# A fused layer norm and gated graph convolution on one core: one load moved, three tiles of the normalisation given to other engines, and the first turns of ScalarE and VectorE in another order

## The chip, the core and the metric

The kernel runs on one core of a Trainium2 chip. The engines of that core that compute here are TensorE (PE in the profile), VectorE (DVE), ScalarE (ACT) and GpSimd (POOL); SyncE (SP) issues nearly all transfers between HBM and SBUF. The metric is the time of one execution on the device in microseconds (us), as the median over runs.

## What is computed

x has 128 graphs of 128 nodes with 128 features, adj one 128x128 matrix of integers for each graph. The weights of the loop relation (W, Wg and two biases) are 128x128 and 1x128.

```python
h = jnp.maximum(_layernorm(x, axis=-1), 0.0)
# _direction(x, W, Wg, b, bg, adj, rel_ids):
    h = x @ W.T
    g = h @ Wg.T
    vals = (h[:, :, None, :] + b) * jax.nn.sigmoid(g[:, :, None, :] + bg)
    onehot = (adj[..., None] == rel_ids).astype(h.dtype)
    return jnp.einsum('bnmr,bmrd->bnd', onehot, vals)
out = _direction(node, W_fwd, Wg_fwd, b_fwd, bg_fwd, adj_mat, rels)              # relations 2 to 40
out = out + _direction(node, W_bwd, Wg_bwd, b_bwd, bg_bwd, adj_t, rels)
out = out + _direction(node, W_loop, Wg_loop, b_loop, bg_loop, adj_t, rel1)      # relation 1
x = x + jax.nn.relu(out)
```

adj holds only 0 and 1 in the drawn inputs, so only relation 1 has entries. The kernel computes that relation alone, sums |adj - 0.5| over all entries, and would run a slow path for all relations behind a branch at the end if the sum said that there are other values. That path doesn't run here.

## The kernel before

The 128 graphs are worked in 32 groups of four. A chunk is two groups: x and adj come in 512 KB chunks (eight graphs, 128x1024 elements), the first chunk of x in two halves. SyncE's queue is written out by hand: x's chunks 0 to 3, then adjacency chunk 0, then x's and adjacency's chunks in turn, and later the stores, each behind a wait for `out_ready`.

For each group g the engines do this:

- VectorE, `row_stats(g)`: two bn_stats passes over two graphs each.
- GpSimd, `coefficients(b)`, once for a batch of groups: variance plus epsilon (`var_eps`), the negated mean (`mean_neg`), and 1/sqrt by a power (`rstd`). The batches are groups 0, 1, 2-3, 4-5, then four groups each (6-9, 10-13, ...); a batch's coefficients wait for the statistics of its last group.
- `normalise(g)`: four 128x128 tiles into `xn`, one instruction each. `POOL_SHARES` says how many of them GpSimd does for the first groups (0, 4, 4, 0, 4, 4), from group 6 on `BATCH_SHARES` (3, 4, 3, 3) by the place in the batch; VectorE does the rest. `xn` has four slots, so group g waits for the turn of group g-4.
- TensorE, `turn_rows(g)`: four transposes into PSUM. ScalarE, `relu_turned(g)`: the relu of it rounded to fp32r, `hT_hi`. VectorE, `low_part(g)`: what the rounding left, `hT_lo`.
- ScalarE, `seed(g)`: writes the biases into the PSUM of the products (128x1024). TensorE, `products(g)`: for each graph hi x w_hi, hi x w_lo, and then lo x w_hi, on top of the biases; it gives h and g at once. The first two kinds wait for `hi_ready` and `seeded`, the last for `hT_ready`.
- ScalarE, `sigmoid(g)`: the gate. VectorE, `messages(g)`: the product h times gate, `vals`.
- ScalarE or GpSimd, `edges(g)`: adjacency to float, `mask`. ScalarE does groups 0 to 3 and each fourth one up to 24.
- TensorE, `aggregate(g)`: mask times vals. VectorE, `output(g)`: relu of it plus x, in place in `x_all`; SyncE stores it.
- ScalarE, `watch(c)`: the sum of |adj - 0.5| of one chunk.

Each engine's order is written by hand. TensorE does, in step t, `turn_rows(t + 2)`, `products(t + 1)`, `aggregate(t)`. GpSimd runs ahead by up to four groups. ScalarE and VectorE have a list of first turns by name and then a loop. Ahead of all that stand the setup of the weights (`turn_weights`, `w_gT`, `w_hi`, `split_weights` for `w_lo`), and matmuls on zeros that keep TensorE busy.

Of the kernel before, what the change touches and what calls it, by code (L numbers as in the profile page):

```python
# [18 lines left out]
def build(nc, x, adj, W_fwd, W_bwd, W_loop, Wg_fwd, Wg_bwd, Wg_loop,  # L19
# [14 lines left out]
    BATCHES = [(0, 0), (1, 1), (2, 3), (4, 5)] + [(g, min(g + 3, GROUPS - 1)) for g in range(6, GROUPS, 4)]  # L34
    BATCH = 4 * GROUP

    POOL_SHARES = (0, 4, 4, 0, 4, 4)

    BATCH_SHARES = (3, 4, 3, 3)
    WATCH_LAG = 3  # L40
# [4 lines left out]
    with ctx:  # L45
# [17 lines left out]
        var_eps = sb("var_eps", [128, BATCH_SLOTS, BATCH])  # L63
        rstd = sb("rstd", [128, BATCH_SLOTS, BATCH])
        mean_neg = sb("mean_neg", [128, BATCH_SLOTS, BATCH])
        minus_half = sb("minus_half", [128, BATCH])
        ident = sb("ident", [128, 128])
        ones = sb("ones", [128, 128])
# [41 lines left out]
        var_ready = sem("var_ready")  # L110
        rstd_ready = sem("rstd_ready")
        mean_ready = sem("mean_ready")
        normed_pool = sem("normed_pool")
        normed_dve = sem("normed_dve")
        turned = sem("turned")
# [86 lines left out]
        def live(g):  # L202
            return 0 <= g < GROUPS
# [11 lines left out]
        def pool_groups(g):  # L215

            return sum(pool_share(k) > 0 for k in range(g))

        def dve_groups(g):
            return sum(pool_share(k) < GROUP for k in range(g))  # L220

        def means_before(b):

# [18 lines left out]
        def _(sp):  # L242
# [19 lines left out]
            load_tile(x_all, x, GROUP, GC, CG - GROUP, x_loaded[0])  # L262
            load_x(1)
            load_x(2)
            load_x(3)
            load_adj(0)
            for c in range(4, LOAD_AHEAD):
                load_x(c)
                load_adj(c - 3)
# [47 lines left out]
        def _(pool):  # L317
# [7 lines left out]
            def coefficients(b):  # L325

                first, last = BATCHES[b]
                s, n = b % BATCH_SLOTS, (last - first + 1) * GROUP
                st = stats[:, s, 0:n // 2, :].rearrange("p k (e f) -> p k e f", e=2)
                pool.wait_ge(stats_ready, b + 1)  # L330
                if b >= BATCH_SLOTS:
                    pool.wait_ge(normed_dve, dve_groups(BATCHES[b - BATCH_SLOTS][1] + 1))
                pool.tensor_scalar(var_eps[:, s, 0:n].rearrange("p (k e) -> p k e", e=2), st[:, :, :, 2],
                                   1.0 / D, EPS, ALU.mult, ALU.add).then_inc(var_ready, 1)
                if means_before(b + 1) > means_before(b):
                    pool.tensor_scalar(mean_neg[:, s, 0:n].rearrange("p (k e) -> p k e", e=2), st[:, :, :, 1],
                                       -1.0, 0.0, ALU.mult, ALU.add).then_inc(mean_ready, 1)
                pool.wait_ge(var_ready, b + 1)
                pool.tensor_tensor(rstd[:, s, 0:n], var_eps[:, s, 0:n], minus_half[:, 0:n], ALU.pow  # L339
                                   ).then_inc(rstd_ready, 1)  # L340

            def normalise(g):

# [50 lines left out]
        def _(act):  # L394
# [21 lines left out]
            def seed(g):  # L416

                s = g % 2
                if g >= 2:
# [3 lines left out]
                    bias_all[:, :, :].rearrange("p a d -> p (a d)").unsqueeze(1)  # L423
                    .to_broadcast([128, GROUP, 2 * D]), ACT.Copy).then_inc(seeded, 1)

            def sigmoid(g):
                s = g % 2
                for graphs, more in parts(g):
# [20 lines left out]
            act.wait_ge(w_turned, 1)  # L449
            nc.scalar.activation(w_gT[:, :], bank[6][:, 128:256], ACT.Copy).then_inc(w_gT_ready, 1)  # L450
            nc.scalar.activation(w_hi[:, 0:D], bank[6][:, 0:D], ACT.Copy).then_inc(w_hi_ready, 1)
            act.wait_ge(bits_set, 1)
            act.wait_ge(bias_ready, 1)
            seed(0)
            act.wait_ge(w_turned, 2)
            nc.scalar.activation(w_hi[:, D:2 * D], bank[7][:, 0:D], ACT.Copy).then_inc(w_hi_ready, 1)
            relu_turned(0)
            seed(1)
            sigmoid(0)
            relu_turned(1)  # L460
            edges(0)
            seed(2)
            relu_turned(2)
            sigmoid(1)
            edges(1)
            edges(2)
            act.wait_ge(half_ready, 1)
            for t in range(1, GROUPS - 1):
                if live(t + 2):
                    relu_turned(t + 2)  # L470
                    seed(t + 2)
                sigmoid(t + 1)
                if t >= WATCH_LAG and (t - WATCH_LAG) % CHUNK == 0:
                    watch((t - WATCH_LAG) // CHUNK)
                if live(t + 2) and mask_by_act(t + 2):
                    edges(t + 2)
                if t == GROUPS - 2:
                    watch(CHUNKS - 2)
# [28 lines left out]
        def _(dve):  # L507
# [84 lines left out]

            row_stats(0)
            row_stats(1)
            normalise(0)
            split_weights(0)
            row_stats(2)
            row_stats(3)
            split_weights(1)
            low_part(0)  # L600
            row_stats(4)
            row_stats(5)
            row_stats(6)
            messages(0)
            low_part(1)
            row_stats(7)
            normalise(3)
            low_part(2)
            messages(1)
            row_stats(8)  # L610
            output(0)
            low_part(3)
            row_stats(9)
            row_stats(10)
            for t in range(2, GROUPS + 1):
                if live(t):
                    messages(t)
                output(t - 1)
                if live(t + 3) and pool_share(t + 3) < GROUP:
                    normalise(t + 3)  # L620
                if live(t + 2):
                    low_part(t + 2)
# [89 lines left out]
        def _(pe):  # L712
# [29 lines left out]
            def turn_rows(g):  # L742
                s = g % 2
                if pool_share(g) > 0:
                    pe.wait_ge(normed_pool, pool_groups(g + 1))
                if pool_share(g) < GROUP:
                    pe.wait_ge(normed_dve, dve_groups(g + 1))
                if g >= 2:
                    pe.wait_ge(hT_ready, g - 1)
# [116 lines left out]
```

## Time and profile before

| | |
|---|---|
| three runs, us | 104.58, 104.6, 105.48 (median 104.6) |
| profiled execution, us | 104.03, of it a span of 102.2 from the first to the last instruction |
| TensorE busy | 95.4 us, 93% of the span; its mean granted clock 0.992 |
| VectorE busy | 90.1 us, 88% |
| ScalarE busy | 88.6 us, 87% |
| GpSimd busy | 85.8 us, 84% |
| moved by transfers | 25.45 MB, mean 249 GB/s |

All four engines are busy for most of the span. An instruction's length and the distance to the next one's start differ: on VectorE and ScalarE the next instruction starts 0.08 to 0.1 us before the last one's recorded end where it has nothing to wait for, and TensorE's matmuls overlap by more. So the working reads distances between starts where it can, and lengths only where there is a single instruction.

### The profile page before, as it was taken

The numbers are of one execution on the slowest core, as the hardware profiler recorded it, in microseconds if no ns is written. First come the engines' busy times: TensorE is split into PE (matmuls) and PEld (weight loads), VectorE is DVE, ScalarE is ACT, GpSimd is POOL, SyncE is SP. The second block draws the span as 40 slices with busy tenths as digits, with TensorE's granted clock in tenths as the row PEclk, the third lists the DMA queues.
The fourth block names the chain that finished last, engine by engine and source line by source line (L and its number), as shares of the span: only waits on it lengthen the run. The fifth ranks groups of instructions, "written<-read, shape, count | busy, mean of one in ns | idle before, by whom it ended". The sixth has DMA issues, their size and how long they took to land.

```text
span 102.2 us, 2493 instructions
## 1 busy us (share of the span) xinstructions
PE 95.4 (93%) x802; PEld 91.3 (89%) x802; DVE 90.1 (88%) x196; ACT 88.6 (87%) x144; POOL 85.8 (84%) x162
## 2 busy tenths in 40 slices
PE   5986899998999999999999999999999999999960
PEld 2655789797999999999999999999999999999950
DVE  2289989999999999999999999999999788777761
ACT  5075498899799998999899989998999989898990
POOL 2188999999999999999999999999999999991000
PEclk9999999999999999999999999999999999999996
DMA  1899999999999999999999999999945150606345
GB/s 50 242 319 292 290 290 290 291 293 294 293 312 298 328 328 331 311 329 322 333 282 317 271 324 316 327 292 313 345 134 157 58 151 28 184 6 205 103 140 168
DMA packets 50288, 25.45 MB, mean 249 GB/s; under 512 B 866, under 2 KB 50276, under 8 KB 50276
## 3 DMA queue, kind: packets, MB, share of 16 engines
q1 hardware_dynamic: 50000, 25.17, 88.5%
q10 hardware_dynamic: 276, 0.13, 0.4%
q8 instruction: 6, 0.10, 0.4%
q14 instruction: 6, 0.05, 0.1%
HBM read 16.91 MB, written 8.39 MB: 247 GB/s over the span
## 4 chain that ended last, share of the span: by engine, by line
PE 71%; POOL 4%; ACT 3%; issue 1%; DVE 0%; POOLq 0%
PE psum L786 23%; PE psum L764 12%; PE psum L769 12%; PE psum L765 12%; PE psum L751 11%; POOL rstd L339 3%; ACT junk L442 2%; POOL xn L352 1%; ACT gate L436 0%; PE psum L811 0%; DVE dist_sum L628 0%; DVE flag L630 0%; POOLq L362 0%
## 5 line engine op out<-in xcount | busy, mean ns | idle before, releaser
L352 POOL TENSOR_SCALAR xn<-x_all,mean_neg,rstd 128x128 f32<-128x128 f32 x101 | 44.7, 454 | 0.7 <-POOL rstd L339 0.4
L764 PE MATMUL psum<-w_hi,hT_hi 128*128 128x256 f32 x128 | 33.8, 299 | 1.3 <-DVE w_lo L589 0.9
L786 PE MATMUL psum<-vals,mask 128*128 128x128 f32 x256 | 33.6, 275 | 0.1
L421 ACT ACTIVATE psum<-bias_all 128x1024 f32<-128x1024 f32 x32 | 33.1, 1035 | 0.3 <-DVE vals L557 0.3
L786 PEld LDWEIGHTS psum<-vals,mask 128*128 128x128 f32 x256 | 31.0, 191 | 0.2 <-issue 0.2
L765 PE MATMUL psum<-w_lo,hT_hi 128*128 128x256 f32 x128 | 31.0, 277 | 0.0
L524 DVE BATCH_NORM_STATS2 stats<-x_all 128x6 f32<-128x256 f32 x64 | 23.9, 418 | 3.2 <-DMA x_all<-in_x 3.0
L764 PEld LDWEIGHTS psum<-w_hi,hT_hi 128*128 128x128 f32 x128 | 24.1, 188 | 2.0 <-DVE w_lo L589 1.1
L557 DVE TENSOR_TENSOR vals<-psum,gate 128x512 f32<-128x512 f32 (+1 forms) x33 | 21.9, 663 | 3.9 <-ACT gate L436 3.3
L339 POOL TENSOR_TENSOR rstd<-var_eps,minus_half 128x16 f32<-128x16 f32 (+2 forms) x11 | 24.5, 2225 | 0.1
L765 PEld LDWEIGHTS psum<-w_lo,hT_hi 128*128 128x128 f32 x128 | 24.2, 189 | 0.0
L567 DVE SCALAR_TENSOR_TENSOR hT_lo<-psum,hT_hi 128x512 fp32r<-128x512 f32 x32 | 21.8, 682 | 1.2 <-ACT hT_hi L414 1.1
L414 ACT ACTIVATE hT_hi<-psum 128x512 fp32r<-128x512 f32 x32 | 19.2, 600 | 3.5 <-PE psum L751 3.5
L582 DVE SCALAR_TENSOR_TENSOR x_all<-psum,x_all 128x512 f32<-128x512 f32 (+1 forms) x33 | 21.7, 662 | 0.1
L436 ACT ACTIVATE gate<-psum 128x512 f32<-128x512 f32 (+1 forms) x33 | 19.4, 587 | 1.7 <-PE psum L769 1.7
L769 PE MATMUL psum<-w_hi,hT_lo 128*128 128x256 f32 x128 | 20.2, 278 | 0.0
L751 PE MATMUL psum<-ident,xn 128*128 128x128 f32 x128 | 19.5, 275 | 0.7 <-POOL xn L352 0.4
L442 ACT ACTIVATE junk<-adj_all,minus_half 128x1024 bf16<-128x1024 int32 x16 | 18.4, 1153 | 0.0
L769 PEld LDWEIGHTS psum<-w_hi,hT_lo 128*128 128x128 f32 x128 | 17.1, 188 | 0.1
L751 PEld LDWEIGHTS psum<-ident,xn 128*128 128x128 f32 x128 | 14.7, 142 | 1.5 <-POOL xn L352 0.8
L363 POOL CAST mask<-adj_all 128x512 f32<-128x512 int32 x22 | 13.3, 611 | 0.0
L541 DVE TENSOR_SCALAR xn<-x_all,stats,rstd 128x128 f32<-128x128 f32 x27 | 8.7, 340 | 0.0
(36 smaller groups left out, 31.3 us busy)
## 6 DMA issues: line engine op xcount, KB each, us to landing
adj_all<-in_adj SPq DMA_DIRECT2D x16, 512.0 KB, 6.8
x_all<-in_x SPq DMA_DIRECT2D x15, 512.0 KB, 6.8
out<-x_all SPq DMA_DIRECT2D x14, 512.0 KB, 6.2
out<-x_all SPq DMA_DIRECT2D x3, 256.0 KB, 2.3
x_all<-in_x SPq DMA_DIRECT2D x2, 256.0 KB, 3.0
out<-x_all ACTq DMA_DIRECT2D x1, 128.0 KB, 2.5
out<-x_all SPq DMA_DIRECT2D x1, 128.0 KB, 2.6
w_raw<-in_L_gnn_W_loop SPq DMA_DIRECT2D x1, 64.0 KB, 2.5
```

Of the source, the lines that this page charges most:

```text
L339: pool.tensor_tensor(rstd[:, s, 0:n], var_eps[:, s, 0:n], minus_half[:, 0:n], ALU.pow).then_inc(rstd_ready, 1)
L352: last = pool.tensor_scalar(xn[:, g % XN, j * D:j * D + D], x_all[:, g * GC + j * D:g * GC + j * D + D], mean_neg[:, b % BATCH_SLOTS, k:k ...
L421: nc.scalar.activation(prod_ps[s].rearrange("p g a d -> p g (a d)"), bias_all[:, :, :].rearrange("p a d -> p (a d)").unsqueeze(1) .to_broa ...
L524: last = nc.vector.bn_stats(stats[:, b % BATCH_SLOTS, ((g - first) * GROUP + j) // 2, :], x_all[:, g * GC + j * D:g * GC + (j + 2) * D].re ...
L557: nc.vector.tensor_tensor(per_graph(vals[:, s, :])[:, some, :], prod_ps[s][:, some, 0, :], per_graph(gate[:, s, :])[:, some, :], ALU.mult) ...
L567: nc.vector.scalar_tensor_tensor(out=hT_lo[:, s, :], in0=hT_ps[s], scalar=0.0, in1=hT_hi[:, s, :].bitcast(FP32), op0=ALU.max, op1=ALU.subt ...
L582: nc.vector.scalar_tensor_tensor(out=cols, in0=sums_ps, scalar=0.0, in1=cols, op0=ALU.max, op1=ALU.add).then_inc(half_out if more else out ...
L751: last = nc.tensor.transpose(hT_ps[s][:, j * N:j * N + N], xn[:, g % XN, j * D:j * D + D], ident[:, :])
L764: nc.tensor.matmul(to, hi, w_hi[:, :], start=False, stop=False, skip_group_check=True)
L765: nc.tensor.matmul(to, hi, w_lo[:, :], start=False, stop=False, skip_group_check=True)
L769: last = nc.tensor.matmul(to, lo, w_hi[:, :], start=False, stop=True, skip_group_check=True)
L786: last = nc.tensor.matmul(to[:, j * D:j * D + D], mask[:, g % MASKS, j * N:j * N + N], vals[:, s, j * D:j * D + D], start=True, stop=True)
```

## The change

- SyncE issues adjacency chunk 0 ahead of x's fourth chunk (chunk 3, groups 6 and 7).
- In group 2 GpSimd normalises two tiles and not four; ScalarE does the other two, as Identity(x * rstd + shift). For it GpSimd computes `shift` = mean_neg * rstd (128x4) behind batch 2's power.
- In group 5 GpSimd normalises three tiles and not four, VectorE the fourth. In group 6 GpSimd normalises four and not three (the last entry of the longer `POOL_SHARES`), VectorE none.
- On ScalarE the second half of `w_hi` comes ahead of `seed(0)`; `seed(2)` comes behind `relu_turned(2)` and not ahead of it; `relu_turned(3)` and `seed(3)` come before `sigmoid(2)`, and the masks of groups 1 to 3 stand elsewhere.
- On VectorE both `split_weights` stand around `normalise(0)`; `normalise(3)` comes ahead of `row_stats(6)` and `messages(1)`; the statistics of groups 6 to 12, the first messages and outputs are interleaved anew.
- TensorE's own order is the same; `turn_rows(2)` waits for ScalarE's tiles too.

```diff
-    POOL_SHARES = (0, 4, 4, 0, 4, 4)
+    POOL_SHARES = (0, 4, 2, 0, 4, 3, 4)
+
+    ACT_GROUP = 2
...
+        def dve_share(g):
+            return 0 if g == ACT_GROUP else GROUP - pool_share(g)
...
             load_x(2)
+            load_adj(0)
             load_x(3)
-            load_adj(0)
...
+                if first == ACT_GROUP:
+                    pool.wait_ge(mean_ready, means_before(b + 1))
+                    pool.wait_ge(rstd_ready, b + 1)
+                    pool.tensor_tensor(shift[:, :], mean_neg[:, s, 0:GROUP], rstd[:, s, 0:GROUP], ALU.mult
+                                       ).then_inc(shift_ready, 1)
...
+            def normalise():
+
+                b = batch_of(ACT_GROUP)[0]
+                act.wait_ge(shift_ready, 1)
+                act.wait_ge(rstd_ready, b + 1)
+                for j in range(pool_share(ACT_GROUP), GROUP):
+                    at = ACT_GROUP * GC + j * D
+                    last = nc.scalar.activation(
+                        xn[:, ACT_GROUP % XN, j * D:j * D + D], x_all[:, at:at + D], ACT.Identity,
+                        bias=shift[:, j:j + 1], scale=rstd[:, b % BATCH_SLOTS, j:j + 1])
+                last.then_inc(normed_act, 1)
...
+            act.wait_ge(w_turned, 2)
+            nc.scalar.activation(w_hi[:, D:2 * D], bank[7][:, 0:D], ACT.Copy).then_inc(w_hi_ready, 1)
             act.wait_ge(bits_set, 1)
             act.wait_ge(bias_ready, 1)
             seed(0)
-            act.wait_ge(w_turned, 2)
-            nc.scalar.activation(w_hi[:, D:2 * D], bank[7][:, 0:D], ACT.Copy).then_inc(w_hi_ready, 1)
...
             edges(0)
+            normalise()
+            sigmoid(1)
+            relu_turned(2)
             seed(2)
-            relu_turned(2)
-            sigmoid(1)
+            relu_turned(3)
             edges(1)
+            seed(3)
+            sigmoid(2)
             edges(2)
+            edges(3)
             act.wait_ge(half_ready, 1)
-            for t in range(1, GROUPS - 1):
+            for t in range(2, GROUPS - 1):
...
             row_stats(1)
+            split_weights(0)
             normalise(0)
-            split_weights(0)
+            split_weights(1)
             row_stats(2)
             row_stats(3)
-            split_weights(1)
             low_part(0)
             row_stats(4)
             row_stats(5)
-            row_stats(6)
             messages(0)
             low_part(1)
+            normalise(3)
+            row_stats(6)
+            messages(1)
+            low_part(2)
             row_stats(7)
-            normalise(3)
-            low_part(2)
-            messages(1)
             row_stats(8)
             output(0)
+            row_stats(9)
             low_part(3)
-            row_stats(9)
+            messages(2)
+            output(1)
+            normalise(5)
+            low_part(4)
             row_stats(10)
...
+                if g == ACT_GROUP:
+                    pe.wait_ge(normed_act, 1)
```

GpSimd from its second batch's tiles on (`xn` is normalise, `var_eps`, `mean_neg` and `rstd` are coefficients). Before:

```order
L352 TENSOR_SCALAR xn<-x_all,mean_neg,rstd 128x128 x4
L333 TENSOR_SCALAR var_eps<-stats 128x8
L336 TENSOR_SCALAR mean_neg<-stats 128x8
L339 TENSOR_TENSOR rstd<-var_eps,minus_half 128x8
L352 TENSOR_SCALAR xn<-x_all,mean_neg,rstd 128x128 x4
L333 TENSOR_SCALAR var_eps<-stats 128x8
L336 TENSOR_SCALAR mean_neg<-stats 128x8
L339 TENSOR_TENSOR rstd<-var_eps,minus_half 128x8
L352 TENSOR_SCALAR xn<-x_all,mean_neg,rstd 128x128 x8
L333 TENSOR_SCALAR var_eps<-stats 128x16
L336 TENSOR_SCALAR mean_neg<-stats 128x16
L339 TENSOR_TENSOR rstd<-var_eps,minus_half 128x16
```

The same stretch of GpSimd in the changed kernel:

```order
L365 TENSOR_SCALAR xn<-x_all,mean_neg,rstd 128x128 x4
L341 TENSOR_SCALAR var_eps<-stats 128x8
L344 TENSOR_SCALAR mean_neg<-stats 128x8
L347 TENSOR_TENSOR rstd<-var_eps,minus_half 128x8
L352 TENSOR_TENSOR shift<-mean_neg,rstd 128x4
L365 TENSOR_SCALAR xn<-x_all,mean_neg,rstd 128x128 x2
L341 TENSOR_SCALAR var_eps<-stats 128x8
L344 TENSOR_SCALAR mean_neg<-stats 128x8
L347 TENSOR_TENSOR rstd<-var_eps,minus_half 128x8
L365 TENSOR_SCALAR xn<-x_all,mean_neg,rstd 128x128 x7
L341 TENSOR_SCALAR var_eps<-stats 128x16
L344 TENSOR_SCALAR mean_neg<-stats 128x16
```

Group 2 has two tiles and the shift ahead of them; groups 4 and 5 together have seven. Behind batch 4's coefficients come eight tiles and not seven.

ScalarE from `relu_turned(1)` on (`hT_hi` is relu_turned, `psum<-bias_all` is seed, `gate` is sigmoid, `mask` is edges). Before:

```order
L414 ACTIVATE hT_hi<-psum 128x512
L405 ACTIVATE mask<-adj_all 128x512
L421 ACTIVATE psum<-bias_all 128x1024
L414 ACTIVATE hT_hi<-psum 128x512
L436 ACTIVATE gate<-psum 128x512
L405 ACTIVATE mask<-adj_all 128x512 x2
L414 ACTIVATE hT_hi<-psum 128x512
L421 ACTIVATE psum<-bias_all 128x1024
L436 ACTIVATE gate<-psum 128x512
L405 ACTIVATE mask<-adj_all 128x512
```

The same stretch of ScalarE in the changed kernel, again from `relu_turned(1)`:

```order
L427 ACTIVATE hT_hi<-psum 128x512
L418 ACTIVATE mask<-adj_all 128x512
L446 ACTIVATE xn<-x_all,shift,rstd 128x128 x2
L461 ACTIVATE gate<-psum 128x512
L427 ACTIVATE hT_hi<-psum 128x512
L434 ACTIVATE psum<-bias_all 128x1024
L427 ACTIVATE hT_hi<-psum 128x512
L418 ACTIVATE mask<-adj_all 128x512
L434 ACTIVATE psum<-bias_all 128x1024
L461 ACTIVATE gate<-psum 128x512
L418 ACTIVATE mask<-adj_all 128x512 x2
```

The seed of group 2 has moved from ahead of group 2's relu to behind group 1's sigmoid and group 2's relu.

VectorE from `low_part(1)` on (`hT_lo` is low_part, `vals` messages, `x_all<-psum` output, `stats` row_stats, `xn` normalise). Before:

```order
L567 SCALAR_TENSOR_TENSOR hT_lo<-psum,hT_hi 128x512
L524 BN_STATS stats<-x_all 128x6 x2
L541 TENSOR_SCALAR xn<-x_all,stats,rstd 128x128 x4
L567 SCALAR_TENSOR_TENSOR hT_lo<-psum,hT_hi 128x512
L557 TENSOR_TENSOR vals<-psum,gate 128x512
L524 BN_STATS stats<-x_all 128x6 x2
L582 SCALAR_TENSOR_TENSOR x_all<-psum,x_all 128x512
L567 SCALAR_TENSOR_TENSOR hT_lo<-psum,hT_hi 128x512
L524 BN_STATS stats<-x_all 128x6 x4
L557 TENSOR_TENSOR vals<-psum,gate 128x512
L582 SCALAR_TENSOR_TENSOR x_all<-psum,x_all 128x512
```

The same stretch of VectorE in the changed kernel:

```order
L597 SCALAR_TENSOR_TENSOR hT_lo<-psum,hT_hi 128x512
L571 TENSOR_SCALAR xn<-x_all,stats,rstd 128x128 x4
L554 BN_STATS stats<-x_all 128x6 x2
L587 TENSOR_TENSOR vals<-psum,gate 128x512
L597 SCALAR_TENSOR_TENSOR hT_lo<-psum,hT_hi 128x512
L554 BN_STATS stats<-x_all 128x6 x4
L612 SCALAR_TENSOR_TENSOR x_all<-psum,x_all 128x512
L554 BN_STATS stats<-x_all 128x6 x2
L597 SCALAR_TENSOR_TENSOR hT_lo<-psum,hT_hi 128x512
L587 TENSOR_TENSOR vals<-psum,gate 128x512
L612 SCALAR_TENSOR_TENSOR x_all<-psum,x_all 128x512
L571 TENSOR_SCALAR xn<-x_all,stats,rstd 128x128
```

Group 3's tiles come right behind `low_part(1)`, the last statistics of batch 4 (group 9) stand alone between `output(0)` and `low_part(3)`, and group 5's tile follows `output(1)`.

## Rows read from the trace of the kernel before

**Rows 1.** The page's chain of waits by engine; GpSimd's wait for VectorE

```profile
PE 71%; POOL 4%; ACT 3%; issue 1%; DVE 0%; POOLq 0%
...
POOL var_eps L333 <- DVE stats L524: 3.4, 2, 3.1
```

**Rows 2.** Stretch, length, busy us of PE, PEld, DVE, ACT, POOL (instructions)

```profile
24.60:46.40 21.80, 21.77 (x193) 21.72 (x193) 21.52 (x46) 20.83 (x35) 21.46 (x39) 1.00 1.12 316
```

**Rows 3.** Timeline of GpSimd: start, length, line, operation, tiles, shapes, count

```profile
19.63 0.21 POOL L333 TENSOR_SCALAR var_eps<-stats 128x16 f32<-128x16 f32 x1
...
23.17 3.12 POOL L352 TENSOR_SCALAR xn<-x_all,mean_neg,rstd 128x128 f32<-128x128 f32 x7 [0.17 <-issue]
...
30.55 2.90 POOL L339 TENSOR_TENSOR rstd<-var_eps,minus_half 128x16 f32<-128x16 f32 x1
...
34.01 3.09 POOL L352 TENSOR_SCALAR xn<-x_all,mean_neg,rstd 128x128 f32<-128x128 f32 x7
...
77.48 3.14 POOL L352 TENSOR_SCALAR xn<-x_all,mean_neg,rstd 128x128 f32<-128x128 f32 x7
```

**Rows 4.** Timeline of TensorE: group 2's first product, later turns

```profile
15.52 0.36 PE L764 MATMUL psum<-w_hi,hT_hi 128*128 128x256 f32 x1
...
24.63 0.66 PE L751 MATMUL psum<-ident,xn 128*128 128x128 f32 x4 [0.42 <-POOL xn L352]
...
35.56 0.60 PE L751 MATMUL psum<-ident,xn 128*128 128x128 f32 x4
...
38.25 0.60 PE L751 MATMUL psum<-ident,xn 128*128 128x128 f32 x4
...
46.36 0.66 PE L751 MATMUL psum<-ident,xn 128*128 128x128 f32 x4
...
79.02 0.60 PE L751 MATMUL psum<-ident,xn 128*128 128x128 f32 x4
```

**Rows 5.** Timeline of GpSimd, first batches

```profile
10.00 0.20 POOL L336 TENSOR_SCALAR mean_neg<-stats 128x8 f32<-128x8 f32 x1
...
11.98 1.74 POOL L352 TENSOR_SCALAR xn<-x_all,mean_neg,rstd 128x128 f32<-128x128 f32 x4 [0.18 <-POOL rstd L339]
...
16.09 3.45 POOL L352 TENSOR_SCALAR xn<-x_all,mean_neg,rstd 128x128 f32<-128x128 f32 x8 [0.17 <-issue]
...
23.17 0.97 POOL L352 TENSOR_SCALAR xn<-x_all,mean_neg,rstd 128x128 f32<-128x128 f32 x2 [0.17 <-issue]
```

**Rows 6.** GpSimd's normalise tiles together; two of VectorE's

```profile
L352 POOL TENSOR_SCALAR xn<-x_all,mean_neg,rstd x101: 438/446/574, 7.9 to 90.2; 128x128 f32<-128x128 f32 x101
...
23.22 0.33 DVE L541 TENSOR_SCALAR xn<-x_all,stats,rstd 128x128 f32<-128x128 f32 x1
...
31.39 0.33 DVE L541 TENSOR_SCALAR xn<-x_all,stats,rstd 128x128 f32<-128x128 f32 x1
```

**Rows 7.** Timeline of ScalarE in the first part

```profile
6.87 0.29 ACT L456 ACTIVATE w_hi<-psum 128x128 fp32r<-128x128 f32 x1
...
12.85 0.63 ACT L405 ACTIVATE mask<-adj_all 128x512 f32<-128x512 int32 x1 [0.93 <-DMA adj_all<-in_adj]
...
14.47 0.60 ACT L414 ACTIVATE hT_hi<-psum 128x512 fp32r<-128x512 f32 x1
...
17.48 1.02 ACT L421 ACTIVATE psum<-bias_all 128x1024 f32<-128x1024 f32 x1
```

**Rows 8.** Timeline of VectorE in the first part

```profile
13.59 1.10 DVE L541 TENSOR_SCALAR xn<-x_all,stats,rstd 128x128 f32<-128x128 f32 x4
...
17.61 0.69 DVE L567 SCALAR_TENSOR_TENSOR hT_lo<-psum,hT_hi 128x512 fp32r<-128x512 f32 x1
18.21 1.43 DVE L524 BATCH_NORM_STATS2 stats<-x_all 128x6 f32<-128x256 f32 x4
```

**Rows 9.** Timeline of SyncE's transfers being issued

```profile
11.03 1.74 SPq L244 DMA_DIRECT2D x_all<-in_x  x1
12.81 1.74 SPq L244 DMA_DIRECT2D adj_all<-in_adj  x1
```

More of the change, by code:

```diff
@@ L65, in build @@
         mean_neg = sb("mean_neg", [128, BATCH_SLOTS, BATCH])
+        shift = sb("shift", [128, GROUP])
         minus_half = sb("minus_half", [128, BATCH])
@@ L112, in build @@
         mean_ready = sem("mean_ready")
+        shift_ready = sem("shift_ready")
+        normed_act = sem("normed_act")
         normed_pool = sem("normed_pool")
@@ L217, in pool_groups @@
             return sum(pool_share(k) > 0 for k in range(g))
+        def dve_share(g):
+            return 0 if g == ACT_GROUP else GROUP - pool_share(g)
         def dve_groups(g):
-            return sum(pool_share(k) < GROUP for k in range(g))
+            return sum(dve_share(k) > 0 for k in range(g))
         def means_before(b):
@@ L602, in _ @@
             row_stats(5)
-            row_stats(6)
             messages(0)
             low_part(1)
+            normalise(3)
+            row_stats(6)
+            messages(1)
+            low_part(2)
             row_stats(7)
-            normalise(3)
-            low_part(2)
-            messages(1)
             row_stats(8)
             output(0)
+            row_stats(9)
             low_part(3)
-            row_stats(9)
+            messages(2)
+            output(1)
+            normalise(5)
+            low_part(4)
             row_stats(10)
-            for t in range(2, GROUPS + 1):
+            messages(3)
+            output(2)
+            row_stats(11)
+            low_part(5)
+            row_stats(12)
+            for t in range(4, GROUPS + 1):
                 if live(t):
@@ L618, in _ @@
                 output(t - 1)
-                if live(t + 3) and pool_share(t + 3) < GROUP:
+                if live(t + 3) and dve_share(t + 3) > 0:
                     normalise(t + 3)
@@ L745, in turn_rows @@
                     pe.wait_ge(normed_pool, pool_groups(g + 1))
-                if pool_share(g) < GROUP:
+                if g == ACT_GROUP:
+                    pe.wait_ge(normed_act, 1)
+                if dve_share(g) > 0:
                     pe.wait_ge(normed_dve, dve_groups(g + 1))
```

## The prediction

> **What bounds the kernel now.** I read the page's chain of waits first, then the busy times by stretch, then the timelines of TensorE and GpSimd side by side. The chain ends on TensorE for 71% of the span, and the next engine in it is GpSimd with 4% [rows 1]; its pieces are the power and the tiles just ahead of TensorE's steady part. From 24.6 to 46.4 us TensorE is busy all the time, but GpSimd (21.46 of 21.80 us) and VectorE (21.52) nearly are too [rows 2]. So which engine sets the pace has to be read from the turns.
>
> A batch of four groups has a fixed rhythm on GpSimd: coefficients (with one 2.9 us power), then 13 tiles and three masks. The tiles of a batch's first two groups start at 23.17, 34.01 and, four batches later, 77.48 us [rows 3]: (77.48 - 23.17) / 5 = 10.86 us a batch. TensorE turns the first group of these batches at 24.63, 35.56, 46.36 and, again three later, 79.02 [rows 4]: 54.39 / 5 = 10.88 us. Left alone TensorE takes 2.69 us a group (35.56 to 38.25), 10.76 us a batch. So TensorE looks like the bound, but what it does each batch is catch up with GpSimd by 0.1 us and wait for it again. Three tiles take 1.3 us and more from 34.01 and 77.48, and end just ahead of the turns at 35.56 and 79.02. In the whole trace GpSimd waited for VectorE's statistics only twice, 3.1 us at the start and once 0.3 us [rows 1]. **GpSimd's line, from its first group on to group 27, sets the time**; after it TensorE runs free to the end, and ScalarE's last gate and the last sums of |adj| come behind TensorE's last products. So every 0.1 us that GpSimd starts batch 4 earlier is 0.1 us of the end, up to where another engine has no room.
>
> **The change, on GpSimd's line.** Before, coefficients(4) start at 19.63 and eight tiles of groups 4 and 5 (16.09 + 3.45) end just ahead of it [rows 3, 5]. It waited for nobody before that since its second batch, so its line moves by what is taken off and put on:
> - Group 2: two tiles fewer. Four take 1.74 us (11.98), so 0.435 each: -0.87.
> - The new instruction shift, 128x4, two waits ahead of it. No row of it exists. The nearest is mean_neg at 10.00, 0.20 us [rows 5]; GpSimd's own gap between a power and the tiles behind it is 0.17 us [rows 3]. Nothing is its lower bound only if it hid in that gap; above I put 0.20 + 0.17 = 0.37. I take 0.20.
> - VectorE's four tiles of group 3 came at 13.59 [rows 8], beside GpSimd's tiny coefficients. Now they come right behind low_part(1), near 12.3, beside GpSimd's two tiles of group 2. GpSimd's tile takes 446 ns in the median and 574 at most [rows 6], and the long ones are those that meet a VectorE tile: the pair at 23.17 took 0.97 and not 0.88 us beside the tile at 23.22. Four such meetings cost 0 to 4 x 0.128 = 0.51. Two or three of them will meet: 0.25.
> - Group 5: one tile fewer, -0.43.
>
> Sum: -0.87 + 0.20 + 0.25 - 0.43 = -0.85. Coefficients(4) could start at 18.78, the tiles of group 6 at 23.17 - 0.85 = 22.32.
> - Group 6: four tiles and not three, +0.435, but VectorE's tile beside them is gone, which cost that pair 0.09 [rows 5, 6]: -0.10. Net +0.34.
>
> **So GpSimd's line is 0.51 us earlier from group 7 on** (bounds: with shift at 0 and no meeting 0.96, with 0.37 and 0.51 it is 0.08). TensorE turns group 6 at 22.32 + 1.74 + 0.06 = 24.12 and not 24.63: 0.51 too. Both keep their distance, so the rhythm of 10.86 goes on, and turn 26 comes near 78.5. The end moves by the same 0.5.
>
> **What has to be there in time.**
> - Statistics of group 9, for coefficients(4) at 18.78. Before, they are the first two of the four passes at 18.21 (1.43 for four), so done at 18.9 [rows 8]. Now: group 3's tiles 12.35 to 13.4, row_stats(6) to 14.1, messages(1) 0.6, low_part(2) 0.6 to 15.3, row_stats(7) and (8) 1.4 to 16.7, output(0) 0.6, row_stats(9) to 18.0 (0.60 for a 128x512 pass with the next behind it, 17.61 to 18.21, and 0.35 for one statistics pass [rows 8]). Room: 0.8 us.
> - x's fourth chunk, for row_stats(6) at 13.4. The first adjacency is seen at 12.85, and one transfer behind another is 1.78 us apart [rows 7, 9]. The two change places: the adjacency is there at 11.1, x's chunk at 12.85. Room: 0.5. It spares ScalarE its wait of 0.93 us, but aggregate(0) comes behind turn(2), so that alone is worth nothing.
> - ScalarE's two tiles. No row has such a pass. A 128x128 from PSUM takes 0.29 (6.87), a 128x512 one 0.60 (14.47) [rows 7]: two cost 0.3 (overlapped) to 1.2. With shift at about 12.2 they are done near 12.8, at worst 13.4; GpSimd's half comes at 13.3. ScalarE waits there for products(1) anyway, which end near 13.3.
> - The reordered turns. products(0) no longer wait for the second w_lo but for relu, about 0.3 us earlier, and products(1) and turn(2) follow, to 13.4. It is lost again: seed(2) stood ahead of relu_turned(2) and sigmoid(1), and now stands behind both, each of which follows TensorE. sigmoid(1) 13.5, relu 14.1, seed 14.6 to 15.6 (1.02 [rows 7]). products(2) start at 15.6; before 15.52 [rows 4]. Worth 0, bounds -0.2 to +0.3.
> - From there to turn(6) TensorE took from 15.52 to 24.21 before (24.63 less 0.42 idle, named after GpSimd's tiles [rows 4]), 0.9 of it waits. It has three products, three aggregations, two turns: 0.44 + 1.36 + 0.89 = 2.69 each. Products(2), aggregate(1), turn(4) to aggregate(3) are then 1.4 + 0.9 + 2 x 2.69 + 0.1 = 7.8 us: ready for turn(6) at 23.4 without waits, at 24.2 with those of before. GpSimd releases it at 24.12. So TensorE's early part, better or a little worse, costs nothing.
> - VectorE gets group 5's tile and gives up group 6's: 0 in sum, and it is about 0.4 ahead of before at messages(4).
>
> By the Trainium skill ("SBUF — State Buffer", section "SBUF: two separate sides") VectorE and GpSimd lock one port pair for a whole instruction. The trace shows meetings that cost 0.13 at most, and the tile at 31.39 takes 0.33 us inside the power of 30.55 to 33.45, not held at all [rows 3, 6].
>
> **The rivals.**
> 1. *Forecast, 0.60.* GpSimd's line shorter by 0.51, TensorE follows. Own range 0.25 to 0.75.
> 2. *Hidden, 0.14.* Coefficients(4) wait for group 9's statistics. It has the reordered VectorE for it (they now stand behind output(0), low_part(2) and so behind relu_turned(2)), and against it 0.8 us of room. With the extra tile of 0.34, all is gone if they come at 19.3 and not 18.0. Time: as before, 104.6.
> 3. *More, 0.16.* Shift and the meetings cost next to nothing: 0.96 less 0.1 to 0.2 for the shift. The executed time falls by 0.8, to 103.8. TensorE's own rate forbids more: at 10.78 it would be at the next turns as early as GpSimd.
> 4. *Slower, 0.10.* VectorE's new tile of group 5 falls, near 19.9, into the power of about 19.3 to 22.1. If a power held it until its end, VectorE would be 2.2 us late: low_part(4), a statistics pair and messages(3) are 2.0 us, to 24.3, aggregate(3) takes 0.9 behind it, and turn(6) comes at 25.2 and not 24.63. VectorE's passes (four of 0.60, a statistics pair 0.68, 0.26 for a tile, 2.7 us a group) catch up slowly, so 0.6 us stay: 105.2. It decides from about 1.2 us of holding. The row at 31.39 speaks against it: no holding there at all.
> By the Trainium skill's rule just named this rival is what one would get; the trace's 0.33 us disagrees with it for this power.
>
> **The numbers.** The sum is against the profiled execution: 104.03 us in all, 102.2 of span. It gives 103.5 and a span of 101.7. The three runs have a median of 104.6, 0.6 above the profiled one, so the forecast as a median is 104.6 - 0.5 = 104.1. Rival 3 gives 103.8, rival 2 104.6, rival 4 105.2. The range of 8 in 10 leaves out the far ends of 3 and most of 4: 103.4 to 104.9. One per cent, 1.05 us, is about what a measurement of this kernel tells from no change (the three runs lie 0.9 apart). The forecast is below that. Faster by over 1% (under 103.55) needs the end of rival 3, 0.10; slower by over 1% (over 105.65) the worse half of rival 4 or something unseen, 0.07; the rest, 0.83, within 1%.
>
> **What the changed profile would show.** GpSimd's 16-column var_eps at 18.8 (right between 18.5 and 19.1), with no idle ahead of it; if it has idle named after VectorE's statistics, rival 2. The shift at 0.2 us, and GpSimd's two tiles of group 2 at 0.5 and over each. products(2) at 15.5 to 15.7 behind ScalarE's seed. TensorE's turn of group 6 at 24.1 with idle ahead of it, named after GpSimd's tiles, and group 26's at 78.5. VectorE's tile near 19.9 at 0.33 us. The forecast is wrong if turn 26 is over 0.3 us from 78.5, or if the stretch from 25 us on no longer has GpSimd's tiles ending just ahead of each fourth turn.

## The result and the profile after

The changed kernel takes 105.22 us in the median of 22 runs (104.74 to 106.13), the kernel before 104.59 us in 22 runs beside them (104.03 to 105.48). The ratio is 1.0067, with a 95% interval of 1.0048 to 1.0086: slower by 0.7%. The forecast was 104.1 us, with a range from 103.4 to 104.9. The profiled execution of the changed kernel has a span of 103.5 us.

The start went as forecast and the steady part did not. GpSimd in the changed kernel, on its timeline (start, length, engine, line, operation, tiles, shapes, count):

```profile
6.55 0.20 POOL L341 TENSOR_SCALAR var_eps<-stats 128x4 f32<-128x4 f32 x1 [0.71 <-DVE stats L554]
...
12.36 0.20 POOL L352 TENSOR_TENSOR shift<-mean_neg,rstd 128x4 f32<-128x4 f32 x1
12.54 0.97 POOL L365 TENSOR_SCALAR xn<-x_all,mean_neg,rstd 128x128 f32<-128x128 f32 x2
13.59 0.33 POOL L341 TENSOR_SCALAR var_eps<-stats 128x8 f32<-128x8 f32 x1
...
19.09 0.21 POOL L341 TENSOR_SCALAR var_eps<-stats 128x16 f32<-128x16 f32 x1
...
22.64 3.46 POOL L365 TENSOR_SCALAR xn<-x_all,mean_neg,rstd 128x128 f32<-128x128 f32 x8 [0.17 <-issue]
```

Coefficients(4) start at 19.09 and not at 19.63 [rows 3]. The first of these lines shows that this execution got its second batch's statistics late, at 6.55; before it was at 6.18:

```profile
6.18 0.21 POOL L333 TENSOR_SCALAR var_eps<-stats 128x4 f32<-128x4 f32 x1 [0.29 <-DVE stats L524]
```

That line is from the timeline of the kernel before. What differs is when the second half of x's first chunk lands, which no edit touches. Counted from there, coefficients(4) come after 12.54 us and not after 13.45: 0.91 earlier.

TensorE's turns of groups 6, 11 to 14 and 26 in the changed kernel, on its timeline:

```profile
24.43 0.66 PE L792 MATMUL psum<-ident,xn 128*128 128x128 f32 x4 [0.39 <-POOL xn L365]
...
38.33 0.60 PE L792 MATMUL psum<-ident,xn 128*128 128x128 f32 x4
...
41.10 0.60 PE L792 MATMUL psum<-ident,xn 128*128 128x128 f32 x4
...
43.86 0.60 PE L792 MATMUL psum<-ident,xn 128*128 128x128 f32 x4
...
46.63 0.60 PE L792 MATMUL psum<-ident,xn 128*128 128x128 f32 x4
...
79.83 0.60 PE L792 MATMUL psum<-ident,xn 128*128 128x128 f32 x4
```

Group 6 is turned at 24.43, 0.20 earlier than before [rows 4]; group 26 at 79.83, 0.81 later. Between them a group takes 2.77 us each time. Before, it took 2.69 in most groups and 2.72 in the mean of all twenty. GpSimd is no longer what TensorE waits for. Its tiles of groups 22 and 23:

```profile
66.16 3.03 POOL L365 TENSOR_SCALAR xn<-x_all,mean_neg,rstd 128x128 f32<-128x128 f32 x7
```

The first three of these end at about 67.5, and TensorE turns group 22 at 68.77. TensorE has 1.3 us of its own to do before it gets there, and in the stretch from 24.6 to 46.4 us it is busy for all of it, as before [rows 2]:

```profile
24.60:46.40 21.80, 21.80 (x190) 21.80 (x190) 21.50 (x46) 20.45 (x34) 21.46 (x39) 1.00 1.12 312
```

So the same instructions of TensorE, in the same order, at a granted clock of 1.00 in both, take longer. The page's groups tell which, first the changed kernel, then the one before (line, engine, operation, out<-in, shapes, count | busy us, mean ns | idle before):

```profile
L827 PE MATMUL psum<-vals,mask 128*128 128x128 f32 x256 | 33.6, 275 | 0.0
L806 PE MATMUL psum<-w_lo,hT_hi 128*128 128x256 f32 x128 | 32.0, 282 | 0.0
...
L810 PE MATMUL psum<-w_hi,hT_lo 128*128 128x256 f32 x128 | 20.7, 281 | 0.0
```

```profile
L786 PE MATMUL psum<-vals,mask 128*128 128x128 f32 x256 | 33.6, 275 | 0.1
...
L765 PE MATMUL psum<-w_lo,hT_hi 128*128 128x256 f32 x128 | 31.0, 277 | 0.0
```

The aggregations (`vals,mask`) have not changed in length, the products have. Within one group, on TensorE's timelines around 40 us, first the kernel before and then the changed one:

```profile
39.60 0.62 PE L769 MATMUL psum<-w_hi,hT_lo 128*128 128x256 f32 x4
40.05 1.05 PE L786 MATMUL psum<-vals,mask 128*128 128x128 f32 x8
40.94 0.60 PE L751 MATMUL psum<-ident,xn 128*128 128x128 f32 x4
```

```profile
39.73 0.64 PE L810 MATMUL psum<-w_hi,hT_lo 128*128 128x256 f32 x4
40.21 1.05 PE L827 MATMUL psum<-vals,mask 128*128 128x128 f32 x8
41.10 0.60 PE L792 MATMUL psum<-ident,xn 128*128 128x128 f32 x4
```

Four products take 0.45 us before and 0.48 us after; eight passes of the aggregation 0.89 in both. Taken from the starts of single matmuls in the trace, a product follows the last one after 113 ns before (118 ns in the first groups, and later in two or three groups behind each short wait of TensorE). In the changed kernel the mean of a group is 119.2 to 120.2 ns, in every group. Twelve products a group make 12 x 6.5 ns = 0.08 us, and that is 2.77 against 2.69.

What could do that? The diff has one more line of effect than its instructions. `shift` is set aside among the SBUF tensors ahead of `ident` and the weights. It has 16 bytes a partition, it takes 32, and so everything behind it lies 32 bytes further on. In the built programs `w_hi` starts at byte 184512 of its partition before and at 184544 after, `w_lo` 1024 behind it; `hT_hi` stays at 155776. The tiles of `hT_hi` and `hT_lo` lie 512 bytes apart. `w_hi` and `w_lo` are what the products stream, `hT_hi` and `hT_lo` what is loaded as weights for them.

**Theory A**: the place of the streamed operand in SBUF sets the step of the products. **Theory B**, its rival: the new order of work makes TensorE's products meet other work of ScalarE, VectorE and GpSimd, and that slows them.

### The profile page after: what moved, and what is told of

Same layout as the page of the kernel before. It is cut to its first block, busy times and chain, and to the rows that moved or that the text cites. A ratio compares the mean times of both kernels' runs of the same rounds, so it can differ in the third digit from the quotient of the medians.

```text
span 103.5 us, 2497 instructions
## 1 busy us (share of the span) xinstructions
PE 97.2 (94%) x802; PEld 93.3 (90%) x802; DVE 90.6 (88%) x196; ACT 89.9 (87%) x146; POOL 84.9 (82%) x161
## 4 chain that ended last, share of the span: by engine, by line
PE 71%; POOL 4%; ACT 2%; issue 1%; DVE 0%
PE psum L827 22%; PE psum L810 13%; PE psum L806 13%; PE psum L805 12%; PE psum L792 11%; POOL rstd L347 3%; ACT junk L467 2%; POOL xn L365 1%; ACT gate L461 0%; PE psum L852 0%; DVE dist_sum L667 0%; DVE flag L669 0%
## 5 line engine op out<-in xcount | busy, mean ns | idle before, releaser
L365 POOL TENSOR_SCALAR xn<-x_all,mean_neg,rstd 128x128 f32<-128x128 f32 x99 | 43.5, 457 | 0.5 <-issue 0.3
L805 PE MATMUL psum<-w_hi,hT_hi 128*128 128x256 f32 x128 | 34.7, 302 | 1.0 <-ACT psum L434 0.4
L806 PE MATMUL psum<-w_lo,hT_hi 128*128 128x256 f32 x128 | 32.0, 282 | 0.0
L810 PE MATMUL psum<-w_hi,hT_lo 128*128 128x256 f32 x128 | 20.7, 281 | 0.0
L810 PEld LDWEIGHTS psum<-w_hi,hT_lo 128*128 128x128 f32 x128 | 17.6, 188 | 0.0
L571 DVE TENSOR_SCALAR xn<-x_all,stats,rstd 128x128 f32<-128x128 f32 x27 | 9.2, 357 | 0.0
```

The costliest lines, as they stand in the source:

```text
L365: last = pool.tensor_scalar(xn[:, g % XN, j * D:j * D + D], x_all[:, g * GC + j * D:g * GC + j * D + D], mean_neg[:, b % BATCH_SLOTS, k:k ...
L805: nc.tensor.matmul(to, hi, w_hi[:, :], start=False, stop=False, skip_group_check=True)
L806: nc.tensor.matmul(to, hi, w_lo[:, :], start=False, stop=False, skip_group_check=True)
L810: last = nc.tensor.matmul(to, lo, w_hi[:, :], start=False, stop=True, skip_group_check=True)
```

## The experiments

All are compared with the kernel before, run beside them on the same chip in the same rounds.

### The place alone, added to the kernel before

```diff
         mean_neg = sb("mean_neg", [128, BATCH_SLOTS, BATCH])
+        spare = sb("spare", [128, 4])
         minus_half = sb("minus_half", [128, BATCH])
```

> The kernel before, with one unused tensor of 128x4 floats set aside where the changed kernel sets aside shift; no instruction differs. It moves w_hi and w_lo 32 bytes on, from an address that is a multiple of 64 bytes (184512) to one that is not (184544). Theory A, address: TensorE's products step by 119.5 to 120.2 ns as in the changed kernel and not by 113.3, a group takes 2.77 us and not 2.69, GpSimd's tiles no longer end just ahead of the turns. From turn 6 at 24.63: 20 groups of 2.767 us to turn 26 at 79.97 (before 79.02), and 0.4 more behind it: 1.3 us slower than before, about 105.9. Theory B, the order of work (TensorE meets ScalarE's and VectorE's work at other moments): no change, 104.6, steps of 113.3 ns.

Measured: 106.43 us, ratio 1.0158 (1.0126 to 1.019), half a microsecond more than expected. The products step by 120 ns in nearly all groups. TensorE's timeline:

```profile
38.09 0.64 PE L770 MATMUL psum<-w_hi,hT_lo 128*128 128x256 f32 x4
38.57 1.05 PE L787 MATMUL psum<-vals,mask 128*128 128x128 f32 x8
39.46 0.60 PE L752 MATMUL psum<-ident,xn 128*128 128x128 f32 x4
```

Four products take 0.48 us, as in the changed kernel. Not one instruction differs from the kernel before; theory B can't explain this run.

A second run narrows it to the two weight tensors:

```diff
+        spare = sb("spare", [128, 8])
         w_hi = sb("w_hi", [128, 2 * D], FP32R)
         w_lo = sb("w_lo", [128, 2 * D], FP32R)
+        spare_2 = sb("spare_2", [128, 8])
```

> The kernel before with 32 unused bytes right ahead of w_hi and 32 behind w_lo, so that only w_hi and w_lo leave their multiple of 64; ident, the raw weights and bias_all stay at multiples of 64. Theory A, that it is the address of what the products stream: as the run with the 16-byte tensor, about 105.9, steps of 119.5 to 120.2 ns. If ident, bias_all or another tensor behind does it: 104.6.

Measured: 106.24 us, ratio 1.0167 (1.0135 to 1.0199), steps of 119 to 120 ns. `ident` and `w_raw` kept their places here, so they have no part in it. `bias_all` did not: it lies 64 bytes further on in this run. But the products read only `w_hi`, `w_lo`, `hT_hi` and `hT_lo`.

### The changed kernel with the old places

```diff
-        shift = sb("shift", [128, GROUP])
...
         rel_id = sb("rel_id", [128, NREL])
+        shift = sb("shift", [128, GROUP])
```

> The changed kernel with the tensor shift set aside behind all others, so that every other tensor has the address it has before; no instruction differs. Theory A, address: products step by 113.3 and 117.8 ns as before, GpSimd's line sets the pace again, and what the change gave there (its tiles of group 7 ended at 26.10 and not 26.29) shows at the end: 104.4, about 0.2 faster than before and 0.9 faster than the changed kernel. Theory B, order of work: 105.2 as the changed kernel, steps of 119.5 to 120.2 ns.

Measured: 103.57 us, ratio 0.9912 (0.9879 to 0.9945), 0.8 us less than the 104.4 of theory A. The steps are 113 and 118 ns again, and GpSimd's tiles end just ahead of each batch's turn again. Its line and TensorE's turn of group 26 on the timelines:

```profile
22.51 3.45 POOL L365 TENSOR_SCALAR xn<-x_all,mean_neg,rstd 128x128 f32<-128x128 f32 x8 [0.17 <-issue]
...
77.20 3.15 POOL L365 TENSOR_SCALAR xn<-x_all,mean_neg,rstd 128x128 f32<-128x128 f32 x7
```

```profile
78.70 0.65 PE L792 MATMUL psum<-ident,xn 128*128 128x128 f32 x4
```

So the edits that were meant give 0.9%, and the 32 bytes take 1.6%. By these two runs the whole result is accounted for: 0.9912 x 1.0158 = 1.0069, and 1.0067 was measured.

### Which places are good

64 bytes set aside for shift where the change has it:

> The changed kernel with shift set aside as 128x16 floats (64 bytes a partition) at the place it has, four columns used. w_hi and w_lo are 64 bytes further on than before and again at a multiple of 64. Theory A, with a multiple of 64 bytes as what matters: as the run with shift set aside last, 104.4. If it is the address as such, or what lies 32 bytes apart in other tensors, it is 105.2. Theory B: 105.2.

Measured: 104.79 us, ratio 0.9998 (0.9975 to 1.0021), steps of 118 to 119 ns. Better than 32 bytes, not as good as the old place. So a multiple of 64 bytes isn't all. Next, 192 bytes on:

```diff
+        spare = sb("spare", [128, 48])
         w_hi = sb("w_hi", [128, 2 * D], FP32R)
```

> The changed kernel with shift set aside last and 192 unused bytes ahead of w_hi, so that w_hi stands at 184704: a multiple of 64 and of 128, 384 past a multiple of 512; hT_hi stays at 128 past one. If every multiple of 128 is as good as before's address (192 past a multiple of 512) or better: products step by 113 ns, 103.6 or less. If the step gets longer with the distance from hT_hi, as the three seen so far could be read (64 bytes: 113 and 118; 96: 120; 128: 118 to 119): 118 ns or more, 104.8 or more.

Measured: 105.23 us, ratio 1.0048 (1.0019 to 1.0078), steps of 120 ns: a multiple of 128 is as bad as the 32 bytes. The run that tells its own address from its place beside the weights:

```diff
         xn = sb("xn", [128, XN, GC])
+        spare = sb("spare", [128, 16])
         hT_hi = sb("hT_hi", [128, 2, GC], FP32R)
```

> The changed kernel with shift set aside last and 64 unused bytes ahead of hT_hi, so that hT_hi, hT_lo and all behind them, w_hi and w_lo too, are 64 bytes further on. w_hi has the address of the run with 64 bytes for shift (184576), but its distance to the weights hT_hi and hT_lo is that of before. Theory C, w_hi's own address counts: products step by 118 to 119 ns as in that run, 104.8. Theory D, its place against what is loaded as weights at the same time counts: 113 ns, 103.6.

Measured: 104.08 us, ratio 0.993 (0.9903 to 0.9956). `w_hi` is where it was in the run with 64 bytes for shift, but the steps are 113 ns in 15 of 32 groups and 118 in the others, and not 118 to 119 in all. TensorE's timeline, in two of the 15:

```profile
47.59 0.62 PE L811 MATMUL psum<-w_hi,hT_lo 128*128 128x256 f32 x4
48.05 1.05 PE L828 MATMUL psum<-vals,mask 128*128 128x128 f32 x8
...
50.29 0.62 PE L811 MATMUL psum<-w_hi,hT_lo 128*128 128x256 f32 x4
50.74 1.05 PE L828 MATMUL psum<-vals,mask 128*128 128x128 f32 x8
```

Four products take 0.45 to 0.46 us. So the address of `w_hi` as such is not what counts, and theory D, the distance, is left. One thing this run does not separate: everything set aside behind `hT_hi` moved with it, `vals` and `mask` too. The median is 0.5 us above that with both at the old places, which was taken on another chip; the ratios lie 0.2% apart and their intervals overlap. The share of 118 ns groups is a little larger (17 of 32 against 13). Why is left open.

Three more distances were run on the version with three tiles in group 6 (below; 103.31 us). That version has the old distance, 64. The steps are means of a group, read from the starts of single matmuls; the table leaves out the first groups and the last.

> The changed kernel with shift last and three tiles in group 6 (103.31 us, products stepping by 113 and 118 ns), and 448 unused bytes ahead of w_hi: w_hi and w_lo stand at the same remainder of 512 as hT_hi and hT_lo (distance 0). Distances seen: 64 bytes 113 and 118 ns; 96, 120; 128, 118 to 119; 256, 120. If what costs is that the streamed operand and the weights being loaded fall on different places of a 512 byte pattern, distance 0 is as good or better: 113 ns or less, 103.3 or less. If the two collide when they are at the same place, it is the worst: 120 ns or more, 104.8 or more.

> As the run with three tiles in group 6 (103.31 us), with 128 unused bytes ahead of w_hi: distance 192 from hT_hi's remainder of 512. If the pattern repeats every 128 bytes (192 is like 64): 113 and 118 ns, 103.3. If 64 is a single good place: 118 to 120 ns, 104.6 to 105.

> As the run with three tiles in group 6 (103.31 us), with 256 unused bytes ahead of w_hi: distance 320. If the pattern repeats every 128 or 256 bytes (320 is like 64): 113 and 118 ns, 103.3. Else 118 to 120 ns, 104.6 to 105.

| distance of w_hi from hT_hi, remainder of 512 bytes | steps of the products, ns | kernel and time, us | ratio |
|---|---|---|---|
| 0 | 119 to 120 | three tiles in group 6: 104.89 | 1.004 (1.0019 to 1.0061) |
| 64 | 113, 118 behind waits | the same: 103.31 | 0.9867 (0.9826 to 0.9907) |
| 96 | 119 to 120 | changed kernel: 105.22 | 1.0067 (1.0048 to 1.0086) |
| 128 | 118 to 119 | changed kernel: 104.79 | 0.9998 (0.9975 to 1.0021) |
| 192 | 114 in most groups, also behind waits | three tiles in group 6: 103.35 | 0.9895 (0.9854 to 0.9936) |
| 256 | 120 | changed kernel: 105.23 | 1.0048 (1.0019 to 1.0078) |
| 320 | 113, 118 | three tiles in group 6: 103.44 | 0.9909 (0.988 to 0.9937) |

The run at 0 came out as its second guess had it (the same place for both is bad), the run at 320 as its first. The run at 192 has a step of its own, and a time within 0.1 us of that at 64. 256 is like 0, and 320 is like 64: as far as these seven go, the pattern repeats every 256 bytes. The good distances, 64, 192 and 320, are the odd multiples of 64; 0, 96 and 256 are the worst. That the weight load of the next product and the stream of the present one get into each other's way fits this (TensorE's loads and matmuls are both busy for all of the 21.80 us above), but no run here shows it; what stands is the table.

### The parts of the intended change

> The changed kernel with shift set aside last, and group 6 normalised as before: three tiles by GpSimd, one by VectorE behind row_stats(11). If GpSimd's line sets the time, as the prediction has it, its tiles of group 7 end 0.34 us earlier and the end moves with them: 0.3 faster than the run with four tiles (103.57), 103.2 to 103.3. If TensorE alone sets the time once products step by 113 ns, or VectorE has no room for the tile: the same or slower, 103.6 and over.

The edit, on the changed kernel with shift last:

```diff
-    POOL_SHARES = (0, 4, 2, 0, 4, 3, 4)
+    POOL_SHARES = (0, 4, 2, 0, 4, 3, 3)
...
             row_stats(11)
+            normalise(6)
             low_part(5)
```

Measured: 103.31 us, ratio 0.9867 (0.9826 to 0.9907), the lowest median of all kernels here. GpSimd's line:

```profile
22.26 3.14 POOL L365 TENSOR_SCALAR xn<-x_all,mean_neg,rstd 128x128 f32<-128x128 f32 x7 [0.17 <-issue]
```

Seven tiles end at 25.40, and eight at 25.96 in the run above with shift last: 0.56 earlier, of which 0.25 is the earlier start. The medians differ by 0.26 us where 0.3 was expected. Counted from coefficients(1), TensorE turns group 26 after 72.02 us and not after 72.26. So the traces and the medians have the fourth tile on GpSimd in group 6 as a loss of about a quarter of a microsecond; the intervals of the two ratios overlap, so the times alone don't prove it.

> The kernel before with the first adjacency chunk loaded ahead of x's fourth, and nothing else. The prediction's step: aggregate(0) stands behind turn(2), which waits for GpSimd's tiles, so the early adjacency is worth nothing: as before, 104.7 within 0.3, the first mask at 11.9 and not 12.85. Rival: masks and seeds of ScalarE come earlier and products(3), which waited for seed(3), too; TensorE still waits for GpSimd at turn 6, so no more than 0.1.

Measured: 105.6 us, ratio 1.0068 (1.0031 to 1.0106): slower, and the expectation missed it. VectorE's timeline:

```profile
12.91 0.77 DVE L524 BATCH_NORM_STATS2 stats<-x_all 128x6 f32<-128x256 f32 x2 [1.71 <-DMA x_all<-in_x]
```

In the old order `row_stats(6)` stands ahead of `messages(0)` and `low_part(1)`. It needs x's fourth chunk, which now comes one transfer later. The last products of group 1 wait on TensorE for the low part behind it, and GpSimd's coefficients(4) wait for group 9's statistics, until 21.59 us. From the list of waits of this run, and from the timelines of TensorE and GpSimd:

```profile
DVE stats L524 <- DMA x_all<-in_x: 5.2, 3, 2.1
...
PE psum L769 <- DVE hT_lo L567: 1.6, 1, 1.6
...
14.93 1.22 PE L769 MATMUL psum<-w_hi,hT_lo 128*128 128x256 f32 x4 [1.56 <-DVE hT_lo L567]
16.80 1.75 PE L786 MATMUL psum<-vals,mask 128*128 128x128 f32 x8
...
21.59 0.21 POOL L333 TENSOR_SCALAR var_eps<-stats 128x16 f32<-128x16 f32 x1 [1.62 <-DVE stats L524]
```

TensorE's clock has a part in it. Behind the wait of 1.56 us the granted clock is 0.50, which is the level of 1.2 GHz, from 15 to 18 us, where it was 1.00 before, and the eight passes of aggregate(0) take 1.59 us (16.80 to 18.39) and not 0.89. But that is not the whole cost: six of the eleven runs have a mean granted clock of 0.993 or more, and their median is 105.3 us.

I had worked out this wait for the changed order, where x's fourth chunk is there in time, and not for the old one. The early adjacency alone costs 0.7%. In the changed kernel, with VectorE's new order, VectorE has no wait for that chunk; what the early adjacency is worth there was not run.

> The kernel before with only the new shares: GpSimd two tiles in group 2 and ScalarE two (ahead of edges(0)), three in group 5, four in group 6, the shift set aside last; loads and the orders of ScalarE and VectorE as before. The prediction's sum by GpSimd's line holds if its coefficients(4) start 12.5 to 12.7 us behind coefficients(1) (before 13.45, changed 12.54) and the time falls by 0.5 or more, to 104.2 or less, most of what the full change gives at the old addresses (103.57). Rival: without the new order VectorE brings the statistics of group 9 or the low part of group 2 too late: 104.5 or more.

Measured: 104.3 us, ratio 0.9983 (0.9959 to 1.0007). GpSimd's timeline:

```profile
19.73 0.21 POOL L341 TENSOR_SCALAR var_eps<-stats 128x16 f32<-128x16 f32 x1 [0.45 <-DVE stats L550]
```

Neither theory's number was met: the time lies between 104.2 and 104.5. Coefficients(4) come 12.78 us behind coefficients(1) (19.73 - 6.95). GpSimd would have been there 0.45 us sooner and waits for group 9's statistics. So the shares alone open 1.12 us of room (13.45 - 12.33, the 12.33 being 12.78 - 0.45), and VectorE's old order closes 0.45 of it. The changed kernel, where VectorE's and ScalarE's orders and the load order are new, has no such wait. This is the prediction's rival 2, in the kernel where VectorE was not reordered.

## Why the prediction was wrong

- **The step that failed**: "Left alone TensorE takes 2.69 us a group", carried over to the changed kernel without a doubt, since TensorE's own order is the same. It was 2.77, by the place of `w_hi` and `w_lo`. "After it TensorE runs free" and "the rhythm of 10.86 goes on" fall with it: 4 x 2.77 = 11.07 us a batch is longer than GpSimd's 10.86. The diff shows the line that does it (`shift = sb(...)` in the middle of the tensors), and the prediction has no term for where tensors lie, which puts it at nothing. None of the four rivals had it; rival 4 was slower for another reason. Why the distance sets the step stays open.
- **What TensorE does before the change** was read too simply. "Catch up with GpSimd by 0.1 us and wait for it again", each batch, is seen in the starts of single matmuls at turns 14 and 22, with 0.08 and 0.04 us, and not at turns 10, 18 and 26. The larger part of what is above 2.69 us a group comes behind the waits: seven of the twenty groups from turn 6 on step by 118 ns and take 0.05 us longer each, 0.35 of some 0.55 us. The mean of 10.88 us a batch was right, its parts were not.
- **The sum on GpSimd's line** was right. Coefficients(4) were to start 12.60 us behind coefficients(1) (18.78 - 6.18) and did after 12.54. By terms: shift 0.20 taken, 0.20 measured; two tiles of group 2 0.97 and not 0.87, and the var_eps behind them 0.33 and not 0.20, so meeting VectorE's tiles cost 0.23 where 0.25 was taken. The tile taken off group 5 gave 0.43, as forecast. Group 7's tiles ended at 26.10, 19.55 behind coefficients(1), against 20.11 before: 0.56, forecast 0.51.
- **What it is worth at the end**, with the places as before: 0.9% (0.55 to 1.2%), so 0.9 us by the ratio and 1.1 us between the medians of 103.57 and 104.68, where 0.5 was forecast. As a change of the median, 0.5 was too small. On the profiled executions, counted from coefficients(1), group 26 is turned 72.84 us later before and 72.26 later with the change: 0.58. The profiled execution of the kernel before was the quickest of its runs (104.03, the lowest of 22), with the earliest second landing of x in any trace here, so a sum made against it alone has this much play.
- **Statistics of group 9**: no wait in the changed kernel, as forecast.
- **ScalarE's two tiles**: 0.88 us together, within 0.3 to 1.2, and hidden. **products(2)** behind the seed: forecast 15.6, measured 15.94, which is 15.57 after taking off the 0.37 us late start; the rows on ScalarE and TensorE:

```profile
12.59 0.88 ACT L446 ACTIVATE xn<-x_all,shift,rstd 128x128 f32<-128x128 f32 x2
13.79 0.60 ACT L461 ACTIVATE gate<-psum 128x512 f32<-128x512 f32 x1 [0.32 <-PE psum L810]
14.29 0.59 ACT L427 ACTIVATE hT_hi<-psum 128x512 fp32r<-128x512 f32 x1
14.76 1.03 ACT L434 ACTIVATE psum<-bias_all 128x1024 f32<-128x1024 f32 x1
```

```profile
15.94 0.36 PE L805 MATMUL psum<-w_hi,hT_hi 128*128 128x256 f32 x1 [0.40 <-ACT psum L434]
```

- **Rival 4**, a tile of VectorE held by GpSimd's power, did not happen. VectorE's new tile lies inside the power of 19.57 to 22.47 and takes its usual time. The Trainium skill's rule on the shared port pair ("SBUF — State Buffer", section "SBUF: two separate sides") has the pair held for a whole instruction, against those of VectorE's instructions that use it; whether this tile is one, no run shows. Read as a hold for the whole power, the rule is not what the trace shows here:

```profile
20.05 0.33 DVE L571 TENSOR_SCALAR xn<-x_all,stats,rstd 128x128 f32<-128x128 f32 x1
```

- **The load order** was taken as worth nothing by itself. In the changed kernel no wait names it; alone it costs 0.7%, and that dependence was not named.

## What to carry to other kernels

Look where a new tensor is set aside, not only at what is done with it: a 16-byte tensor in the middle of an allocation moved the streamed weights by 32 bytes, and that cost 1.6% of this kernel, more than the intended change gave. When an engine without any changed instruction gets slower by a constant few per cent, compare the step between like instructions first, and test the placement with an unused tensor in the old kernel. A sum made against one profiled execution should be counted from an event behind the first transfers, whose landing moves from run to run.

## What the runs showed of the hardware that I had not expected

- The step of fp32r matmuls with 256 streamed columns, each with its weight load, depends on where the streamed operand lies in its partition against the weights: 113 ns at 64 or 320 bytes apart, 114 at 192, 118 to 119 at 128, 119 to 120 at 0, 96 and 256 (remainders of 512 bytes). The aggregations, whose tensors kept their places, stayed at 0.89 us for eight passes.
- At 64 and 320 bytes there are two steps, 113 and 118 ns. In the steady part the 118 ns ones come in runs of one to three groups. Nearly every run starts at a wait of TensorE, of 0.01 to 0.13 us; two in the run with the shares alone start where the trace shows none. What starts and ends them is open. At 192 bytes there are no such runs: a group starts with steps of 120, 117 and 116 ns and goes on with 113.
- Where VectorE's and GpSimd's normalise tiles meet, now the one and now the other is longer. In the changed kernel VectorE's tile started at 12.76 and GpSimd's at 12.98, and GpSimd's took 0.53 us (usually 0.45). With shift last GpSimd's started at 12.87 and VectorE's at 12.96, and VectorE's took 0.44 (usually 0.34). GpSimd's tiny instructions were slowed too (var_eps 0.33 against 0.20).
- The second half of x's first chunk was seen on VectorE between 5.33 and 6.09 us in executions with the same loads ahead of it.
